# Placing x in a graph network's entry stage: two more blocks before the first layer, behind a wait for all look-ups

## The chip, the cores and the metric

The kernel runs on one core of a Trainium2 chip. The metric is the device time of one execution in microseconds (us), here the median of three runs. The core's engines are TensorE (PE), VectorE (DVE), ScalarE (ACT), GpSimd (POOL) and SyncE (SP); each has an instruction queue of its own, and all wait for each other only through semaphores and at the barrier between two stages.

## What is computed

Four graph convolutions on 50,000 nodes with 96 features, and 50,000 edges sorted by their destination; each is added to its input and layer-normalised. The part that matters here is the first one:

```python
edge_index = jnp.stack([src, dst])
x = _layernorm(x + _L0_gnn_ref(x, L0_gnn_W, L0_gnn_b, src, dst), axis=-1)
...
def _L0_gnn_ref(x, W, b, src, dst):
    inv_sqrt_out = jnp.where(deg_out > 0, jax.lax.rsqrt(deg_out), 0.0)
    inv_sqrt_in = jnp.where(deg_in > 0, jax.lax.rsqrt(deg_in), 0.0)
    h = x @ W
    coef = inv_sqrt_out[src] * inv_sqrt_in[dst]
    msg = h[src] * coef[:, None]
    agg = jax.ops.segment_sum(msg, dst, num_segments=N_NODES)
    return agg + b
```

The three further layers (a max-aggregating pair, a softmax aggregation, an attention layer) are not touched by the change.

## The kernel before, in words

**Tiling.** The 50,000 edges are padded to 128 x 391. A "tile" is one column of 128 edges (or of the 128 node rows that belong to it), a "block" is `Q = 8` tiles; there are `NCH = 49` blocks, 0 to 48 (the last one has 7 tiles), and one extra single-tile block 49 (`FIX`). The big buffer `k.O` holds, for each of the 392 tiles, the node rows of x to which the layer's result is added. A row is placed there by an indirect DMA of POOL, one per tile (128 rows of 384 bytes), with the node numbers in `k.nidx` as its list.

**Stages.** The program is a row of stages: numbering, entry, layer0, layer1 twice, layer2, layer3. Each is a `Block` in which every engine has a program of its own. At a block's end each engine's queue runs a DRAIN instruction and then meets the others at a barrier; no engine starts the next stage before all have arrived. The trace gives these under the line of the stage's `with ctx:` (L527 for entry, L862 for the end of layer0).

**Entry** (from line 512). POOL places blocks 0 to `LATE - 1` = 42 of x in `k.O` (line 642), eight blocks in flight on eight semaphores `placed`. From block `HELD_BACK` = 36 on it first waits until the tallies on PE are done, since the upper part of `k.O` serves as scratch before that: columns of blocks 36 to 42 hold one-hot matrices (`spare`), and those from block 43 up hold `turned_hi`, the transposed one-hot matrices that the look-ups read. A look-up is two matmuls on PE (line 852, reading `turned_hi`) and one instruction on DVE (`look`, line 729) that picks the wanted entries and increments `looked`; there are `2 * TILES` = 128 of them, three behind each of the first 42 blocks that DVE scales and two behind block 42. Meanwhile SP loads each block of x into a ring of four buffers, DVE scales it (line 774), and SP stores it to the table `xs` (lines 615 and 622). SP's program ends when all stores have landed.

**Layer0** (from line 857). POOL first places the blocks that entry left, `LATE` to 49 (line 961), and then gathers the rows of `xs` for the blocks from `RAW` = 8 on into a ring of four slots, one indirect DMA per tile (line 973). Blocks 0 to 7 come by SP from `xraw` (line 937). Before the gathers of block c, POOL waits for what frees its slot:

```python
                if SLOTS <= c < NCH:
                    pool.wait_ge(turned_s, fours(c - SLOTS + 1))
                    pool.wait_ge(counted, c - SLOTS + 1)
                    pool.wait_ge(chained, c - SLOTS + 2)
                    pool.wait_ge(kept[s], 16 * (c // SLOTS))
```

`chained` counts blocks whose running sums are done on DVE (`chain`, line 1004), so `c - SLOTS + 2` means that the chain of block c - 3 has ended; `kept` counts the landed stores of a slot's sums (SP, line 946). DVE's order in each step t is `chain(t)`, then `join(t - 1)` and `factors(t - 1)`. `join` waits for the block's placement (from entry's semaphores below `LATE`, from layer0's above), adds the bias in `k.O` (line 1025), adds PE's product and takes the norm's statistics. From block 8 on a chain begins with line 996, which waits for the block's gathers.

Of the kernel before, what the change touches and what calls it, by code (L numbers as in the profile page):

```python
# [7 lines left out]
F16 = mybir.dt.float16  # L8
# [5 lines left out]
Q = 8  # L14
N_NODES = 50000
N_EDGES = 50000
RAW = 8
LATE = 43
K = 391
KP = K + K % 2  # L20
NP = 128 * K
# [34 lines left out]
def tiles(c):  # L56

    return min(Q, K - c * Q) if c < NCH else 1


def cols(c):
    first = c * Q if c < NCH else FIX
    return slice(first, first + tiles(c))
# [148 lines left out]
def segment_kernel(nc, x, src_k, dst_ext, dst_before, starts, edge_k, W0, b0, W1m, W1e, W1r, b1, W2m, W2e, W2r, b2,  # L212
                   Wg, bg, Wa, att, ba, out):
    ctx = ExitStack()
    with ctx:
# [46 lines left out]
        numbering(nc, k, first, src_k, dst_ext, x, xraw)  # L262
        k.O = sb("O", [128, K + 1, D])
        entry(nc, k, first, x, dst_before, starts, xs)
        layer0(nc, k, second, first, x, xraw, xs, h0, t1, r1, W0, b0, W1m, W1r, b1)
        first.close()
# [245 lines left out]
def entry(nc, k, stage, x, dst_before, starts, xs):  # L512
# [9 lines left out]
    HELD_BACK = 36  # L522
    TILES = RAW * Q
# [3 lines left out]
    with ctx:  # L527
        def sb(name, shape, dt=F32):
            return ctx.enter_context(nc.sbuf_tensor("en_" + name, shape, dt))
# [4 lines left out]
        def sem(name):  # L534
            return stage.sem("en_" + name)
# [22 lines left out]
        table = sb("table", [128, 2, 2, KP], F16)  # L558
        low_bits = sb("low_bits", [128, K], I32)
        y = sb("y", [128, YRING, Q, YW])  # L560
        spare = k.O[:, HELD_BACK * Q:LATE * Q, :].rearrange("p a b -> p (a b)")
        turned_hi = k.O[:, LATE * Q:K, :].rearrange("p a b -> p (a b)")[:, 0:TILES * 64].bitcast(F16)
        halves = lambda at, n: spare[:, at // 2:(at + n) // 2].bitcast(F16)
        width = 2 * HOT * KP
        hots = lambda c: min(HOT, K - c * HOT) if c < NHOT else 1
# [26 lines left out]
        looked = sem("looked")  # L592
# [12 lines left out]
        @block.sync  # L605
        def _(sp):
            sp.dma_start(dprev[:, :], dst_before).then_inc(loaded, 16)
            sp.dma_start(ends[:, 0, :], starts[0:1, :].to_broadcast([128, 128])).then_inc(loaded, 16)
            sp.dma_start(ends[:, 1, :], starts[1:2, :].to_broadcast([128, 128])).then_inc(loaded, 16)

            def load(c):
                u = c % YRING
                if c >= YRING:
                    sp.wait_ge(x_out[u], 16 * (c // YRING))
                sp.dma_start(y[:, u, 0:tiles(c), 0:D], rows(x, c)).then_inc(x_in[u], 16)

            for c in range(YRING - 1):
                load(c)
            for c in range(NCH):
                sp.wait_ge(scaled, c + 1)  # L620
                sp.wait_ge(headed, c + 1)
                sp.dma_start(rows(xs, c), y[:, c % YRING, 0:tiles(c), :]).then_inc(x_out[c % YRING], 16)
                if c + YRING - 1 < NCH:
                    load(c + YRING - 1)
            for u in range(YRING):
                sp.wait_ge(x_out[u], 16 * rounds(NCH, u, YRING))

        @block.gpsimd
        def _(pool):
            pool.memset(after[:, :], 1.0).then_inc(consts, 1)  # L630
            pool.wait_ge(consts, 1)
            pool.affine_select(out=after[:, :], in_=after[:, :], compare_op=ALU.is_gt, fill=0.0,
                               base=0, pattern=[[-1, 128]], channel_multiplier=1).then_inc(consts, 1)
            for c in range(LATE):
                if c >= RING:
                    pool.wait_ge(placed[c % RING], 128 * (c // RING))
                if c == HELD_BACK:
                    pool.wait_ge(s_tallied, NHOT)
                    pool.wait_ge(tallied, NHOT + 1)
                for q in range(tiles(c)):  # L640
                    at = cols(c).start + q
                    pool.indirect_dma_start(k.O[:, at, :], None, x,  # L642
                                            bass.IndirectOffsetOnAxis(k.nidx[:, at:at + 1], 0))\
                        .then_inc(placed[c % RING], 16)
# [212 lines left out]
def layer0(nc, k, stage, old, x, xraw, xs, hist, t1, r1, W0, b0, Wm, Wr, b):  # L857
# [4 lines left out]
    with ctx:  # L862
# [6 lines left out]
        def sem(name):  # L869
            return stage.sem("l0_" + name)  # L870
# [22 lines left out]
        raw_in = [sem(f"raw_in{s}") for s in range(SLOTS)]  # L893
        placed = [k.sem(f"l0_placed{c}") for c in range(LATE, NCH + 1)]
        kept = [sem(f"kept{s}") for s in range(SLOTS)]
# [24 lines left out]
        @block.sync  # L920
        def _(sp):
            clear(sp, old.sems)
            sp.dma_start(w0[:, :], W0).then_inc(weights, 16)
            sp.dma_start(w[0:D, 0:D], Wm).then_inc(weights, 16)
            sp.dma_start(w[0:D, D:2 * D], Wr).then_inc(weights, 16)
            sp.dma_start(w[D:D + 1, D:2 * D], b).then_inc(weights, 16)
            sp.dma_start(b0r[:, :], b0.to_broadcast([128, D])).then_inc(weights, 16)
            raw_rows = xraw.rearrange("(p c q) d -> p c q d", p=128, q=Q)

            def load_raw(c):  # L930
                s = c % SLOTS
                if c >= SLOTS:
                    sp.wait_ge(turned_s, fours(c - SLOTS + 1))
                    sp.wait_ge(counted, c - SLOTS + 1)
                    sp.wait_ge(chained, c - SLOTS + 2)
                    sp.wait_ge(kept[s], 16 * (c // SLOTS))
                sp.dma_start(tile(c)[:, :, 0:D], raw_rows[:, c, :, :]).then_inc(raw_in[s], 16)

            for c in range(SLOTS):
                load_raw(c)  # L940
            for t in range(LAST + 1):
                if t >= 2 and t + 2 < RAW:
                    load_raw(t + 2)
                if t < NCH - 1:
                    sp.wait_ge(chained, t + 1)
                    sp.dma_start(sums_of(hist, t), tile(t)).then_inc(kept[t % SLOTS], 16)
                c = t - 2
                if c >= 0:
                    u, n = c % 2, width(c)
                    sp.wait_ge(taken, c + 1)  # L950
                    sp.dma_start(part_of(t1, c), tr_out[:, u, 0:n, 0:D]).then_inc(stored[u], 16)
                    sp.dma_start(part_of(r1, c), tr_out[:, u, 0:n, D:2 * D]).then_inc(stored[u], 16)
            for u in range(2):
                sp.wait_ge(stored[u], 32 * rounds(NL + 1, u, 2))

        @block.gpsimd
        def _(pool):
            for c in range(LATE, NCH + 1):
                for q in range(tiles(c)):
                    at = cols(c).start + q  # L960
                    pool.indirect_dma_start(k.O[:, at, :], None, x,
                                            bass.IndirectOffsetOnAxis(k.nidx[:, at:at + 1], 0))\
                        .then_inc(placed[c - LATE], 16)
            for c in range(RAW, NL):
# [1240 lines left out]
```

## Time and profile before

| | |
|---|---|
| runs | 3799.91 us median of 3 (3792.94 to 3800.45) |
| the profiled execution | 3788.51 us, of which the span of its instructions is 3786.7 |
| busy over the span | DVE 75%, POOL 71%, PE 49%, ACT 49% |
| entry | from about 157 us to the barrier at 607.7 us |
| layer0 | to the barrier at 1116.4 us |

Times in the rows are microseconds from the span's start, unless marked ns. Register, branch and semaphore instructions don't count as busy; a name with a q (POOLq) is the engine's queue, which runs ahead of the engine. A transfer that POOL issues lands after its row has ended (2.4 to 5.8 us from the issue at line 642).

### The profile page before, as it was taken

To read this page: it belongs to the slowest core of one execution; us is meant where nothing else is said; L and a number is where in the kernel's file an instruction comes from. 1 tells how busy PE (TensorE), PEld (TensorE's weight loads), DVE (VectorE), ACT (ScalarE), POOL (GpSimd) and SP (SyncE) were. 2 spreads that over 40 slices of the span, in tenths; PEclk is the share of its full clock that TensorE was granted. 3 is DMA by queue.
4 is the path that set the end of the run, shared out by engine and by line. 5 is a ranking of instruction groups with operands and counts; after the bars stand their busy time and mean duration, and the time that the engine had idled before them with its cause. 6 is when DMAs were issued, how large, how long until landed. Compare 5 with 4: busy or idle time off the path is not lost. (4 is left out here: it accounts for less than half of the span.)

```text
span 3786.7 us, 39744 instructions
## 1 busy us (share of the span) xinstructions
PE 1847.8 (49%) x8382; PEld 1354.4 (36%) x8382; DVE 2821.7 (75%) x10541; ACT 1853.3 (49%) x3815; POOL 2675.7 (71%) x2760
## 2 busy tenths in 40 slices
PE   5478675888766666744554357888820000000000
PEld 2244313777755555522222157777710000000000
DVE  8899987888866666659999878888755565555555
ACT  8699602776652222225545546666643333333333
POOL 7377776777747777757777477766457777777776
PEclk9899855888878787766666656665655555555555
DMA  2111397666556666646666545555422222222221
GB/s 53 51 41 40 79 295 200 168 166 162 156 139 201 205 205 210 203 131 204 208 202 210 167 156 173 185 171 171 147 82 78 82 77 78 82 74 81 82 73 55
DMA packets 380539, 524.64 MB, mean 139 GB/s; under 512 B 221914, under 2 KB 255983, under 8 KB 380042
## 3 DMA queue, kind: packets, MB, share of 16 engines
q1 hardware_dynamic: 286154, 366.89, 29.3%
q0 software_dynamic: 94144, 155.21, 17.4%
q8 instruction: 69, 1.13, 0.1%
q14 instruction: 172, 1.41, 0.1%
HBM read 230.36 MB, written 291.54 MB: 138 GB/s over the span
## 5 line engine op out<-in xcount | busy, mean ns | idle before, releaser
L1626 POOL DMA_INDIRECT l_G<-t,src x391 | 387.7, 991 | 181.8 <-issue 150.8
L1927 POOL DMA_INDIRECT l_G<-t,src x391 | 373.3, 955 | 168.3 <-issue 107.4
L2161 PE MATMUL l_psR<-l_diag,l_ones 128*128 128x128 f32 x2 | 0.8, 501 | 991.2 <-DVE l_diag L2025 991.2
L1307 POOL DMA_INDIRECT l1a_G<-t,src x391 | 378.8, 969 | 148.3 <-issue 117.3
L1307 POOL DMA_INDIRECT l1b_G<-t,src x391 | 378.4, 968 | 142.8 <-issue 117.9
L1942 POOL DMA_INDIRECT out<-O,nidx x392 | 384.3, 980 | 127.8 <-issue 118.2
L642 POOL DMA_INDIRECT O<-x_pad,nidx x344 | 326.9, 950 | 104.7 <-issue 104.7
L973 POOL DMA_INDIRECT l_G<-xs,src x327 | 311.7, 953 | 99.6 <-issue 96.3
L2161 PEld LDWEIGHTS l_psR<-l_diag,l_ones 128*128 128x128 f32 x2 | 0.5, 310 | 991.3 <-DVE l_diag L2025 991.3
L207 ACT ACTIVATE O<-O,l_shift,l_rstd 128x96 f32<-128x96 f32 x784 | 291.2, 453 | 27.2 <-DVE l_shift L201 26.7
L1480 PE MATMUL l1b_psE<-l1b_G,ident 128*128 128x384 f32 (+1 forms) x198 | 147.1, 845 | 260.3 <-DMA l1b_G<-t,src 260.3
L1982 DVE TENSOR_TENSOR l_e<-l_G,l_to_score 128x8 f32<-128x8 f32 (+3 forms) x51 | 9.3, 183 | 307.6 <-DMA l_G<-t,src 307.6
L1504 PE MATMUL l1a_psP<-l1a_w,l1a_xT 97*128 97x192 f32 x784 | 209.1, 441 | 56.5 <-ACT l1a_xT L1423 56.5
L207 ACT ACTIVATE O<-O,l1b_shift,l1b_rstd 128x96 f32<-128x96 f32 x392 | 146.0, 454 | 162.8 <-DVE l1b_shift L201 162.8
L793 ACT ACTIVATE O<-iota_lo,en_s_from 128x392 f16<-128x392 f16 x391 | 214.1, 654 | 22.8 <-DVE en_s_from L656 22.8
L172 PE MATMUL l_psX<-ident,O 128*96 128x128 f32 x784 | 172.4, 377 | 105.9 <-ACT O L207 82.0
L1504 PEld LDWEIGHTS l1a_psP<-l1a_w,l1a_xT 97*128 97x128 f32 x784 | 189.1, 267 | 73.1 <-ACT l1a_xT L1423 73.1
L2116 ACT ACTIVATE l_psK<-l_dd 128x32 f32<-128x32 f32 (+3 forms) x51 | 10.2, 200 | 371.2 <-DVE l_dd L2002 371.2
L1654 DVE SCALAR_TENSOR_TENSOR l_G<-l_G,cont 128x192 f32<-128x192 f32 x390 | 163.8, 420 | 29.6 <-DMA l_G<-t,src 13.5
L1791 PE MATMUL l_psN<-l_wg,l_vT 97*128 97x96 f32 x784 | 140.2, 352 | 83.5 <-DVE O L1683 60.9
L1480 PEld LDWEIGHTS l1b_psE<-l1b_G,ident 128*128 128x128 f32 x198 | 57.8, 321 | 326.5 <-issue 319.4
L172 PEld LDWEIGHTS l_psX<-ident,O 128*96 128x96 f32 x784 | 124.5, 176 | 133.2 <-ACT O L207 93.2
(351 smaller groups left out, 6480.8 us busy)
## 6 DMA issues: line engine op xcount, KB each, us to landing
h<-l_G SPq DMA_DIRECT2D x96, 392.0 KB, 2.9
t<-l1b_t_out SPq DMA_DIRECT2D x48, 768.0 KB
h<-l_G SPq DMA_DIRECT2D x48, 768.0 KB
xs<-en_y SPq DMA_DIRECT2D x48, 392.0 KB, 4.3
t<-l_t_out SPq DMA_DIRECT2D x48, 392.0 KB, 3.6
l_H<-t SPq DMA_DIRECT2D x48, 392.0 KB, 3.2
en_y<-x_pad SPq DMA_DIRECT2D x48, 384.0 KB, 5.0
t<-l_tr_out SPq DMA_DIRECT2D x48, 384.0 KB
```

The costliest lines, as they stand in the source:

```text
L172: last = pe.transpose(psum[0:D, q * 128:(q + 1) * 128], tile_of(q), ident[:, :])
L207: last = act.activation(out_of(q), tile_of(q), ACT.Identity, bias=shift[:, u, q:q + 1], scale=rstd[:, u, q:q + 1])
L642: pool.indirect_dma_start(k.O[:, at, :], None, x, bass.IndirectOffsetOnAxis(k.nidx[:, at:at + 1], 0))\
L793: made = act.activation(hot_s_lo[:, u, q, :], k.iota_lo[:, :], ACT.Sign, bias=s_from[:, c * HOT + q:c * HOT + q + 1])
L973: pool.indirect_dma_start(tile(c)[:, q, :], None, xs, bass.IndirectOffsetOnAxis(k.src[:, at:at + 1], 0))\
L1307: pool.indirect_dma_start(tile(c)[:, q, :], None, table, bass.IndirectOffsetOnAxis(k.src[:, at:at + 1], 0))\
L1480: pe.matmul(V(c)[:, a:a + n, :], k.ident[:, :], tile(c)[:, a:a + n, :], start=True, stop=False, skip_group_check=True)
L1504: last = pe.matmul(P[:, q, 0:2 * D], xT[:, q * 128:(q + 1) * 128], w[:, :], start=True, stop=True)
L1626: pool.indirect_dma_start(tile(c)[:, q, :], None, table, bass.IndirectOffsetOnAxis(k.src[:, at:at + 1], 0))\
L1654: done = dve.scalar_tensor_tensor(S[:, q, :], before, k.cont[:, at:at + 1], S[:, q, :], ALU.mult, ALU.add)
L1927: pool.indirect_dma_start(tile(c)[:, q, :], None, t4, bass.IndirectOffsetOnAxis(k.src[:, at:at + 1], 0))\
L1942: pool.indirect_dma_start(out, bass.IndirectOffsetOnAxis(k.nidx[:, at:at + 1], 0), k.O[:, at, :], None, bounds_check=NP - 1, oob_is_err=Fa ...
```

## The change

The line between "placed in entry" and "placed in layer0" moves from block 43 to block 45, and the scratch areas keep their old border under a name of their own, `TURNED`. Since blocks 43 and 44 lie on `turned_hi`, POOL waits before block 43 until all 128 look-ups have been counted.

```diff
-LATE = 43
+TURNED = 43
+LATE = 45
...
-        spare = k.O[:, HELD_BACK * Q:LATE * Q, :].rearrange("p a b -> p (a b)")
-        turned_hi = k.O[:, LATE * Q:K, :].rearrange("p a b -> p (a b)")[:, 0:TILES * 64].bitcast(F16)
+        spare = k.O[:, HELD_BACK * Q:TURNED * Q, :].rearrange("p a b -> p (a b)")
+        turned_hi = k.O[:, TURNED * Q:K, :].rearrange("p a b -> p (a b)")[:, 0:TILES * 64].bitcast(F16)
...
                 if c == HELD_BACK:
                     pool.wait_ge(s_tallied, NHOT)
                     pool.wait_ge(tallied, NHOT + 1)
+                if c == TURNED:
+                    pool.wait_ge(looked, 2 * TILES)
                 for q in range(tiles(c)):
```

The same constant `LATE` is the start of layer0's placement loop, the offset of its semaphores `placed`, and the test in `join` that chooses between entry's semaphores and layer0's.

POOL's instructions at the end of entry and the start of layer0, before (O is `k.O`, x_pad is x, and the waits are the semaphores of the kernel's names):

```order
L642 DMA O<-x_pad,nidx 128x96 [waits en_placed2]
L642 DMA O<-x_pad,nidx 128x96 x7
L527 UNCONDITIONAL_BRANCH
L956 UNCONDITIONAL_BRANCH [waits barrier_Pool_Activation_PE_DVE_SP_gather]
L961 DMA O<-x_pad,nidx 128x96 x48
L973 DMA l_G<-xs,src 128x98 [waits l0_chained,l0_kept0,l0_counted,l0_turned_s]
L973 DMA l_G<-xs,src 128x98 x7
```

And of the change, at the same place (its lines stand three further down, those of the stage's end one):

```order
L645 DMA O<-x_pad,nidx 128x96 [waits en_placed2]
L645 DMA O<-x_pad,nidx 128x96 x7
L645 DMA O<-x_pad,nidx 128x96 [waits en_looked,en_placed3]
L645 DMA O<-x_pad,nidx 128x96 x7
L645 DMA O<-x_pad,nidx 128x96 [waits en_placed4]
L645 DMA O<-x_pad,nidx 128x96 x7
L528 UNCONDITIONAL_BRANCH
L959 UNCONDITIONAL_BRANCH [waits barrier_Pool_Activation_PE_DVE_SP_gather]
L964 DMA O<-x_pad,nidx 128x96 x32
L976 DMA l_G<-xs,src 128x98 [waits l0_chained,l0_kept0,l0_counted,l0_turned_s]
L976 DMA l_G<-xs,src 128x98 x7
```

Sixteen placements have moved from behind the barrier to ahead of it, the first of them behind the wait for the look-ups; 48 placements of layer0 have become 32.

## Rows read from the trace of the kernel before

**Rows 1.** Line 527, the end of entry: duration ns min/median/max, start.

```profile
L527 POOLq EVENT_SEMAPHORE  x2: 17/17/17, 607.7 to 607.7; - x2
L527 POOLq DRAIN  x1: 22201/22201/22201, 573.8 to 573.8; - x1
...
L527 DVEq DRAIN  x1: 560/560/560, 605.4 to 605.4; - x1
...
L527 SPq DRAIN  x1: 7/7/7, 607.6 to 607.6; - x1
```

**Rows 2.** Timeline of POOL, end of entry: start, us, instruction [idle before].

```profile
587.86 0.94 POOL L642 DMA_INDIRECT O<-x_pad,nidx  x1 [0.30 <-issue]
608.53 0.94 POOL L961 DMA_INDIRECT O<-x_pad,nidx  x1 [19.73 <-POOLq L527]
```

**Rows 3.** Line 642, 570 to 600 us: duration ns, first and last start.

```profile
L642 POOL DMA_INDIRECT O<-x_pad,nidx x16: 940/944/947, 569.1 to 587.9; - x16
```

**Rows 4.** Timeline of DVE: the last look-up, the last scaling.

```profile
590.41 0.08 DVE L729 DVE_READ_ACCUMULATOR en_picked<-iota_lo,en_s_lo,en_psL 128x1 f32 x1
...
604.35 0.85 DVE L774 TENSOR_TENSOR en_y<-en_y,en_psC 128x672 f32<-128x672 f32 x1 [2.07 <-DMA en_y<-x_pad]
```

**Rows 5.** POOL's other drains: lines 285, 862, 1181 (its second), 1832.

```profile
L285 POOLq DRAIN  x1: 6543/6543/6543, 146.7 to 146.7; - x1
L862 POOLq DRAIN  x1: 4482/4482/4482, 1086.5 to 1086.5; - x1
L1181 POOLq DRAIN  x1: 9701/9701/9701, 2145.1 to 2145.1; - x1
L1832 POOLq DRAIN  x1: 5927/5927/5927, 3780.6 to 3780.6; - x1
L1832 POOLq EVENT_SEMAPHORE  x2: 17/17/17, 3786.6 to 3786.6; - x2
```

**Rows 6.** Timeline of POOL: the last instruction ahead of each of those drains.

```profile
146.93 0.94 POOL L392 DMA_INDIRECT nu_E<-nu_table,nu_first_free  x1 [43.64 <-DMA nu_table<-nu_zero_nodes]
...
1086.73 0.95 POOL L978 DMA_INDIRECT l_F<-h,hrow  x1 [6.19 <-DMA h<-l_G]
...
2145.30 0.94 POOL L1312 DMA_INDIRECT l1b_F<-h1b,hrow  x1 [7.01 <-DMA h1b<-l1b_G]
...
3778.19 0.97 POOL L1942 DMA_INDIRECT out<-O,nidx  x1 [7.48 <-ACT O L207]
```

**Rows 7.** Timeline of POOL: the first gathers of blocks 8, 9 and 10.

```profile
669.54 0.94 POOL L973 DMA_INDIRECT l_G<-xs,src  x1 [0.30 <-PE l_psS L172]
...
679.68 0.95 POOL L973 DMA_INDIRECT l_G<-xs,src  x1 [0.30 <-PE l_psS L172]
...
689.85 0.94 POOL L973 DMA_INDIRECT l_G<-xs,src  x1 [0.30 <-PE l_psS L172]
```

**Rows 8.** Timeline of DVE: the chains of blocks 5 to 9.

```profile
663.28 2.81 DVE L1004 SCALAR_TENSOR_TENSOR l_G<-l_G,cont 128x97 f32<-128x97 f32 x8
...
673.44 2.81 DVE L1004 SCALAR_TENSOR_TENSOR l_G<-l_G,cont 128x97 f32<-128x97 f32 x8
...
683.60 2.81 DVE L1004 SCALAR_TENSOR_TENSOR l_G<-l_G,cont 128x97 f32<-128x97 f32 x8
692.72 0.17 DVE L996 CAST src<-l_G 128x8 int32<-128x8 f32 x1
692.96 2.81 DVE L1004 SCALAR_TENSOR_TENSOR l_G<-l_G,cont 128x97 f32<-128x97 f32 x8
702.09 0.17 DVE L996 CAST src<-l_G 128x8 int32<-128x8 f32 x1
```

**Rows 9.** Line 946, 655 to 690 us: the stores of sums, DMA to landing.

```profile
L946 SPq DMA_DIRECT2D h<-l_G x3: 1263/1406/1468, 658.8 to 677.9; - x3
DMA to landing us min/median/max: 6.7/6.7/6.7
```

**Rows 10.** Waits of POOL in layer0: total us, times, longest.

```profile
POOL l_G L973 <- issue: 96.3, 316, 0.3
POOL O L961 <- POOLq L527: 19.7, 1, 19.7
```

**Rows 11.** Line 973, and what DVE's line 996 waited for (us, times).

```profile
L973 POOL DMA_INDIRECT l_G<-xs,src x327: 940/944/1124, 669.5 to 1079.5; - x164
...
  DMA l_G<-xs,src: 11.9, 10
```

**Rows 12.** Timeline of DVE: its last wait for a gather in layer0.

```profile
1056.84 0.23 DVE L996 CAST src<-l_G 128x8 int32<-128x8 f32 x1 [2.18 <-DMA l_G<-xs,src]
```

## The prediction

> **What bounds the kernel now.** I read the end of entry first, since that is where work is added. The queue instructions of the stage's end [rows 1] show who arrives at the barrier last: SP's drain stands at 607.6 and the barrier opens at 607.7, DVE's drain ends at 606.0 (605.4 + 0.56), and POOL's drain ends at 596.0 (573.8 + 22.2). So SP's last store sets the end of entry, and POOL is 11.6 us early. The timeline of POOL [rows 2] shows the same gap from the engine's side: its last placement ends at 588.8, and it then sits idle for 19.7 us until layer0's first placement at 608.53. The reader should see that these are two different numbers: the engine is free for 19.7 us, but only 11.6 us are left once its queue has drained, because the drain ends 7.2 us behind the last placement (596.0 - 588.8).
>
> Then layer0. POOL issues with no gap but the 0.30 us between two DMAs [rows 10, 11]: 327 gathers from 669.5 to 1079.5 are 1.25 us each, 10.0 us a block. DVE's period is 10.2 us a block while the blocks come from xraw (the chains of blocks 5, 6 and 7 [rows 8]) and 9.4 us once they are gathered (692.72 to 702.09). So POOL has a lead at first and loses 0.6 us of it a block; from the middle of the layer on DVE waits for gathers, 11.9 us in 10 waits [rows 11], the last at 1056.84 [rows 12], close to the layer's end. What makes POOL's stream of gathers earlier against DVE's start of the layer is therefore worth up to 11.9 us, and no more.
>
> **The change part by part.**
>
> *The names.* `TURNED` keeps the scratch areas where they were: nothing.
>
> *The wait for the look-ups.* The last look-up's result is read at 590.41 + 0.08 = 590.5 [rows 4], which is 1.7 us after POOL's last placement of today. The wait holds only what stands behind it on POOL, the 16 moved placements, and nobody in entry waits for these. From the release to the first placement I take 0.5 us, an estimate between the 0.30 of a gap between two DMAs and the 0.8 from the barrier to 608.53 [rows 1, 2].
>
> *Sixteen placements ahead of the barrier.* Sixteen of them start over 18.8 us (569.1 to 587.9 [rows 3]) and the last takes 0.94, so they end at 590.5 + 0.5 + 18.8 + 0.9 = 610.7. That alone is 3.1 us past the 607.6 at which SP arrives. Behind it comes the drain. Its cost is not shown for this place, so I bound it by the drains the trace has [rows 5, 6], each from the end of POOL's last instruction to the end of the drain: 5.4 us after numbering (153.2 - 147.9), 3.3 after layer0 (1091.0 - 1087.7), 8.6 at the second L1181 (2154.8 - 2146.2), 7.3 at the kernel's end (3786.5 - 3779.2), and 7.2 here. I take 7.2, the same queue behind the same kind of placement under the same traffic; the ends are 3.3 and 8.6. The drain does gate the barrier: at the kernel's end POOL's drain ends at 3786.5 and the semaphores follow at 3786.6 [rows 5]. So POOL arrives at 610.7 + 7.2 = 617.9, and layer0 starts 617.9 - 607.6 = **10.3 us later** (6.4 to 11.7). The cover that hid POOL's end, the 11.6 us up to SP's arrival, is used up.
>
> The Trainium skill (PSUM — Partial Sum Buffer, Engine vs sequencer instructions) says that a "drain waits for the engine to go fully idle". Read with POOL's rows alone that would put the arrival at 610.7, and the start 3.1 us later instead of 10.3. The trace disagrees with that reading: the drain ended 7.2 us behind the last row. The Trainium skill (Perfetto Trace Analysis, DMA Instruction — SWDGE) also says that such a row ends when the descriptors are written and not when the data has moved, which fits a tail behind it.
>
> *More traffic beside the last stores of entry.* The 16 transfers run beside SP's last five loads and stores. These may come later, but SP now has 617.9 - 607.6 = 10.3 us of slack: nothing.
>
> *Sixteen placements fewer in layer0.* They free 16 x 1.25 = 20 us of POOL ahead of the gathers. How much of that can be used is set by the slots. Block 8's slot is free once the chain of block 5 has ended, at 663.28 + 2.81 = 666.1 [rows 8] (the store of sums that it also needs was issued at 658.8 and landed 6.7 later, at 665.5 [rows 9]), and its gathers start at 669.54 [rows 7]. With 0.3 us for the release, only 669.5 - 666.4 = 3.1 us can be won; blocks 9 and 10 give the same (679.68 - 676.25 - 0.3 and 689.85 - 686.41 - 0.3). From block 11 on POOL is the slower one again and carries the 3.1 us through to the last wait of DVE, which they shorten, since 3.1 is less than 11.9. The rest of the 20 us becomes a new wait of some 17 us on POOL ahead of block 8. Ends: 0, if the store of sums lands a few us later and frees the slot last, and 3.4, with no release. **I take 3.1 us gained.**
>
> *Blocks 43 and 44 in `join`.* They are joined 400 us later; their placement is hidden either way.
>
> **Sum.** 10.3 - 3.1 = +7.2 us, all of it on the path, since every later stage starts at a barrier. The profiled execution would go from 3788.51 to 3795.7 us; it is 11.4 us below the median of the three runs shown, to which I add the same: 3799.91 + 7.2 = **3807.1 us**, taken as 3807. From the ends, the change is 6.4 - 3.4 = +3.0 to 11.7 - 0 = +11.7 us. About 0.2%, 7.6 us, is what a measurement of this kernel can tell from no change, so the forecast lies just inside it, on the slow side.
>
> **Rivals.**
>
> *The drain has no tail to pay.* If the 7.2 us are a cost of the DMA queue being full of SP's traffic, or pass while POOL sits at the new wait, the start moves by 3.1 only and the sum is 3.1 - 3.1 = 0: 3800 us. For it: the shortest drain shown is 3.3, behind a lone DMA. Against it: the one behind a lone DMA at 2145 took 8.6. With a tail of 3.3 the sum is 6.4 - 3.1 = +3.3, 3803 us; that is the low end of the forecast, not this rival.
>
> *Slower by more.* The gain in layer0 doesn't come. The place is POOL's wait ahead of block 8: the store of sums leaves 0.6 us of room before the chain (665.5 against 666.1 [rows 8, 9]), and it decides from a landing 0.6 us later on; at 3.4 later nothing of the gain is left. With the drain at 7.2 or at 8.6 that is +10.3 or +11.7: 3810 to 3812 us. For it: the small room, three times in a row. Against it: with 16 placements fewer, layer0's first stores meet less traffic.
>
> *Faster.* The gathers come early enough that DVE never waits: -11.9 us. With a start 3.1 us later that is -8.8, 3791 us. It needs POOL to begin block 8 some 12 us before the chain of block 5 ends, which the wait on `chained` excludes, unless the chains themselves come earlier. Against it: DVE is busy through the first eight blocks and does not wait for POOL there. With the full 10.3 it would be -1.6, no change.
>
> *The change doesn't do what it says.* If `looked` reached 128 well before 590, the 16 placements would join the others at 588.8 and end 1.9 us earlier: +5.3, 3805 us. The timeline of DVE excludes it, for the last look-up ends at 590.5.
>
> **How the numbers follow.** The forecast (+3 to +9) has a chance of 0.68, of which 0.31 lies above 7.6 us, since two of the five drains shown would put it there or next to it; no tail 0.12; slower by more 0.14; faster 0.04; the last 0.02. Slower by over 0.2%: 0.31 + 0.14 = 0.45. Faster by over 0.2%: 0.05, the rival's 0.04 and a little scatter. Within 0.2%: the other 0.50. The range starts at 3797 (no tail, on a run at the low end of the three shown) and ends at 3813 (drain 8.6, no gain, and 1 us of the runs' own scatter).
>
> **What the profile after would show.** Right: a gap of about 2 us on POOL ahead of the first placement of block 43 at 591; POOL's last placement ending at 610.7; its drain ending at about 618 and all other queues waiting for it; layer0's first instructions 10 us later; a wait of some 17 us on POOL ahead of block 8; DVE's waits for gathers down from 11.9 to about 9 us; the barrier behind layer0 at 1116.4 + 7.2 = 1123.6. Wrong: the barrier still at 608 to 611 (no tail), the first gather of block 8 more than 1 us after the end of the chain of block 5 (no gain), or a stage after layer0 whose length has changed.

## The result, and the profile after

The change makes the kernel slower: 3806.7 us median of 9 runs (3802.8 to 3812.48), the kernel before 3796.58 us median of 9 (3789.46 to 3800.45). The ratio is 1.0028 with a 95% interval of 1.0018 to 1.0038, so between 6.8 and 14.4 us of 3797; the difference of the medians is 10.1 us. The profiled execution took 3802.8 us, with a span of 3801.0 from its first instruction to its last.

The end of entry (line 528 of the changed kernel) answers to [rows 1]; columns are duration ns min/median/max, first and last start:

```profile
L528 POOLq EVENT_SEMAPHORE  x2: 17/17/17, 619.4 to 619.4; - x2
...
L528 POOLq DRAIN  x1: 21022/21022/21022, 598.3 to 598.3; - x1
...
L528 DVEq DRAIN  x1: 669/669/669, 605.1 to 605.1; - x1
...
L528 SPq DRAIN  x1: 7/7/7, 607.7 to 607.7; - x1
```

SP arrives at 607.7, 0.1 us from where it was. POOL's drain now ends at 598.3 + 21.0 = 619.3, and the barrier opens at 619.4, 11.7 us later than before. The timeline of POOL answers to [rows 2, 7]; columns are start, duration, instruction, [idle time before <- what ended it]:

```profile
591.04 0.95 POOL L645 DMA_INDIRECT O<-x_pad,nidx  x1 [1.69 <-DVE en_picked L732]
...
609.81 0.94 POOL L645 DMA_INDIRECT O<-x_pad,nidx  x1 [0.30 <-issue]
620.21 0.95 POOL L964 DMA_INDIRECT O<-x_pad,nidx  x1 [9.46 <-POOLq L528]
...
678.85 1.03 POOL L976 DMA_INDIRECT l_G<-xs,src  x1 [18.19 <-PE l_psS L173]
...
688.99 1.05 POOL L976 DMA_INDIRECT l_G<-xs,src  x1 [0.35 <-PE l_psS L173]
```

The first moved placement starts at 591.04, 0.8 us behind the end of the last look-up (590.26), and the last one ends at 610.75, as the sum had it. The drain then takes 8.6 us more, not 7.2. In layer0 the 20 us that POOL was relieved of turn into a wait of 18.2 us ahead of block 8. The chains on DVE answer to [rows 8]:

```profile
675.18 2.81 DVE L1007 SCALAR_TENSOR_TENSOR l_G<-l_G,cont 128x97 f32<-128x97 f32 x8
...
685.34 2.81 DVE L1007 SCALAR_TENSOR_TENSOR l_G<-l_G,cont 128x97 f32<-128x97 f32 x8
```

The chain of block 5 ends at 677.99 and that of block 6 at 688.15, and the gathers of blocks 8 and 9 follow 0.86 and 0.84 us behind them: the slots gate POOL now. (The row of the first gather names PE's `l_psS` as what ended the wait. That is inferred. In e3, below, the same wait is put down to the chain on DVE, the distance is 0.85 us, and PE's work on `l_psS` was still running when the gather started.) Against the barrier, the first gather of block 8 comes at 678.85 - 619.4 = 59.4 us, before at 669.54 - 607.7 = 61.8. So 2.4 us of 20 are won. DVE sees nothing of it until block 25, the first whose gathers it had to wait for before. The row is the start of that block's chain (line 996, now 999), before and after:

```profile
855.13 0.39 DVE L996 CAST src<-l_G 128x8 int32<-128x8 f32 x1 [1.51 <-DMA l_G<-xs,src]
```

```profile
865.38 0.17 DVE L999 CAST src<-l_G 128x8 int32<-128x8 f32 x1
```

Counted from the barrier that is 247.4 us before and 246.0 after: the wait is gone, and the chain starts 1.4 us earlier. At the last block's chain the lead is 1.3 us. The gather stream and the end of layer0 answer to [rows 11]:

```profile
L976 POOL DMA_INDIRECT l_G<-xs,src x327: 943/947/1124, 678.9 to 1089.9; - x164
```

```profile
DVE src L999 <- DMA l_G<-xs,src: 11.4, 12, 2.1
```

```profile
L865 POOLq EVENT_SEMAPHORE  x2: 17/17/17, 1126.9 to 1126.9; - x2
```

The last gather starts 10.4 us later than before and the barrier behind layer0 opens 10.5 us later (1126.9 against 1116.4). The code behind this barrier is the same in both kernels. The later barriers of the two profiled executions lie +9.2, +7.6, +12.5 and +14.2 us apart (1649.4 against 1640.2 for the first, the end of the program for the last); they scatter both ways about the 10.1 us that the medians show, and nothing is to be explained there from one execution of each.

### The profile page after: what moved, and what is told of

Its sections match the earlier page's. It is cut to its first block and busy times, and to the rows that moved or that the text cites. A ratio compares the mean times of both kernels' runs of the same rounds, so it can differ in the third digit from the quotient of the medians.

```text
span 3801.0 us, 39745 instructions
## 1 busy us (share of the span) xinstructions
PE 1841.3 (48%) x8382; PEld 1348.9 (35%) x8382; DVE 2824.9 (74%) x10541; ACT 1853.4 (49%) x3815; POOL 2678.3 (70%) x2760
## 5 line engine op out<-in xcount | busy, mean ns | idle before, releaser
L645 POOL DMA_INDIRECT O<-x_pad,nidx x360 | 342.8, 952 | 111.0 <-issue 109.3
L1507 PE MATMUL l1a_psP<-l1a_w,l1a_xT 97*128 97x192 f32 x784 | 201.0, 428 | 56.8 <-ACT l1a_xT L1426 56.8
L2119 ACT ACTIVATE l_psK<-l_dd 128x32 f32<-128x32 f32 (+3 forms) x51 | 10.2, 200 | 372.3 <-DVE l_dd L2005 372.3
L1155 PE MATMUL l_psP<-l_w,l_xT 97*128 97x192 f32 x784 | 167.6, 374 | 7.4 <-ACT l_xT L1092 7.2
```

The costliest lines, as they stand in the source:

```text
L645: pool.indirect_dma_start(k.O[:, at, :], None, x, bass.IndirectOffsetOnAxis(k.nidx[:, at:at + 1], 0))\
L1155: last = pe.matmul(P[:, q // 2, q % 2 * 2 * D:(q % 2 + 1) * 2 * D], xT[:, c % 2, q * 128:(q + 1) * 128], w[:, :], start=True, stop=True)
L1507: last = pe.matmul(P[:, q, 0:2 * D], xT[:, q * 128:(q + 1) * 128], w[:, :], start=True, stop=True)
```

## The experiments

The theory is the prediction's: POOL's drain gates the barrier, and the ring of four slots limits what can be won in layer0. The first four kernels take cost, gain and size apart; e5, e8 and e9 move placements to where the drain stays hidden, and e6 to e9 open the slots; e10 asks what the drain waits for. In the table, "barrier" is the end of entry, "gather 8" the first gather of block 8 counted from it, and "layer0" the time from that barrier to the next, all from the one profiled execution of each. Each ratio is against runs of the kernel before that were made beside it; their medians lie between 3791.9 and 3796.8 us.

| kernel | time against before (95%) | barrier | gather 8 | layer0 |
|---|---|---|---|---|
| before | 1 | 607.7 | 61.8 | 508.7 |
| the change | 1.0028 (1.0018 to 1.0038) | 619.4 | 59.4 | 507.5 |
| e1, one block | 0.9998 (0.9987 to 1.0008) | 608.7 | 59.8 | 507.9 |
| e2, cost alone | 1.0021 (1.0011 to 1.0032) | 619.8 | 61.6 | 510.0 |
| e3, gain alone | 0.9986 (0.9976 to 0.9996) | 607.2 | 59.3 | 509.5 |
| e4, three blocks | one run, 3814.55 us | 630.0 | 59.1 | 507.2 |
| e5, eight hidden | 1.0006 (0.9996 to 1.0016) | 608.0 | 59.5 | 513.9 |
| e6, five slots | 1.0005 (0.9995 to 1.0014) | 605.9 | 62.1 | 513.0 |
| e7, change and five slots | 0.9997 (0.9988 to 1.0006) | 619.2 | 49.2 | 500.7 |
| e8, hidden and five slots | 0.9983 (0.9973 to 0.9992) | 605.7 | 51.8 | 506.9 |
| e9, the same, other scratch | 0.9976 (0.9967 to 0.9986) | 606.3 | 51.9 | 501.7 |
| e10, landings awaited | one run, 3806.08 us | 620.0 | 59.8 | 508.1 |

**e1, one block instead of two**

```diff
-LATE = 45
+LATE = 44
```

> One block (8 placements) moves ahead of the barrier instead of two; the wait for the look-ups stays. Theory (POOL's drain gates the barrier, the slots limit the gain): POOL's last placement ends at about 601, its drain ends 7.2 to 8.6 us later, at 607.9 to 609.3, so the barrier opens 0.3 to 1.7 us later than before; the gathers of block 8 again start right behind the chain of block 5, which gives back 2.4 us. Sum -2.1 to -0.7 us, no change that can be measured. Rival (the placements slow SP's last stores and the first loads of layer0): SP's drain moves to 609 or later and half of the +10 us of the change remains, +5 us.

```profile
L528 POOLq DRAIN  x1: 14472/14472/14472, 594.1 to 594.1; - x1
...
L528 SPq DRAIN  x1: 7/7/7, 607.3 to 607.3; - x1
```

POOL's last placement ended at 600.7 and its drain at 608.6, 7.9 us later, 1.3 us behind SP. The barrier opened 1.0 us later than in the trace of before, inside the theory's 0.3 to 1.7; SP was not slowed (607.3), which the rival needed. The first gather of block 8 came 2.0 us earlier against the barrier, where 2.4 was expected. The time is that of the kernel before: the interval is 4.9 us less to 3.0 us more, which leaves out the rival's +5.

**e2, the cost alone**

```diff
+REST = 43
...
-            for c in range(LATE, NCH + 1):
+            for c in range(REST, LATE):
+                pool.wait_ge(k.early_placed[c % 8], 128 * (c // 8 + 1))
+            for c in range(REST, NCH + 1):
```

> Entry as in the change; layer0 places all of blocks 43 to 49 as the kernel before did, so blocks 43 and 44 are placed twice and POOL has nothing less to do there. Theory: barrier as in the change, 11.7 us later than before, and no gain: the first gather of block 8 comes 11.7 us later, +11.7 us in all. Rival (the cost arises inside layer0, from having the placements gone from there): no more than 5 us of it is left.

The barrier opened at 619.8 and the first gather of block 8 started at 681.4, 61.6 us behind it, as in the kernel before. The whole time is 1.0021 of before, 4.2 to 12.2 us more by the interval, which holds the +11.7 of the theory near its upper end: the cost is there with all of layer0's placements in place, and so arises in entry. The rival falls: at most 5 us of 10 were to remain, and the barrier alone is 12 us late.

**e3, the gain alone**

```diff
-        placed = [k.sem(f"l0_placed{c}") for c in range(LATE, NCH + 1)]
+        placed = [k.sem(f"l0_placed{c}") for c in range(REST, NCH + 1)]
...
-            for c in range(LATE, NCH + 1):
+            for c in range(REST, NCH + 1):
```

with `REST = 45` beside `LATE = 43`, and `join` not waiting for blocks 43 and 44.

> Entry as in the kernel before; layer0 places only blocks 45 to 49. This leaves out the placement of blocks 43 and 44, whose rows of x are missing from the result. Theory: barrier at 607.7 as before; POOL has 20 us less to do and turns 17 to 18 us of it into a wait ahead of block 8, whose gathers start about 0.85 us behind the chain of block 5, 2.4 us earlier than before: -2.4 us. Rival (the slots don't limit it, and POOL's time ahead of the gathers comes off DVE's 11.9 us of waits): -11.9 us.

```profile
666.53 1.04 POOL L974 DMA_INDIRECT l_G<-xs,src  x1 [18.19 <-DVE l_G L1005]
```

The same wait of 18.2 us appears with entry untouched, and gather 8 comes 2.5 us earlier against the barrier. The interval of the times, 0.9976 to 0.9996, is a gain of 1.5 to 9.1 us; it holds the 2.4 of the theory and not the 11.9 of the rival. The profiled layer0 was not shorter, though (509.5 against 508.7 us), so the gain that reaches the end of the layer is shown by the times and not by this trace.

**e4, three blocks**

```diff
-LATE = 45
+LATE = 46
```

> Three blocks (24 placements) ahead of the barrier. Theory: 10.0 us more than the change, all of it on the barrier and none given back: POOL's last placement ends at 620.7, its drain at 627.9 to 629.3, and the first gather of block 8 comes 19 to 20 us later than before. Rival (the drain's tail is room that a longer wait fills, or the gain grows with the placements moved): less than 8 us more than the change.

```profile
L528 POOLq DRAIN  x1: 24196/24196/24196, 605.7 to 605.7; - x1
```

The drain ends at 629.9, 9.2 us behind the last placement (620.7), and gather 8 starts at 689.1, 19.5 us later than before. A third block costs 10.6 us at the barrier, of which 9.9 are its placements and the rest a longer drain, and gains nothing more in layer0. Its one time, 3814.55 us, is 7.9 above the change's median, just under the rival's 8; one run does not decide that, but the barrier does.

**e5, eight placements where the drain stays hidden**

```diff
+HIDDEN = list(range(387, 392)) + list(range(344, 347))
...
+            for at in HIDDEN:
+                if at == LATE * Q:
+                    pool.wait_ge(looked, 2 * TILES)
+                pool.indirect_dma_start(k.O[:, at, :], None, x, bass.IndirectOffsetOnAxis(k.nidx[:, at:at + 1], 0))\
+                    .then_inc(hidden, 16)
```

> Eight placements move ahead of the barrier, but such that POOL's drain ends before SP arrives: first tiles 387 to 391, which lie beyond turned_hi and need no wait, then, behind the wait for the look-ups, tiles 344 to 346. Theory: POOL's last placement ends at 598.5, its drain at 605.7 to 607.7, the barrier opens at 607.7 as before, and block 8's gathers start 2.4 us earlier: -2.4 us, which the times can hardly show. Rival (any placement beside SP's last stores costs): barrier at 609 or later.

POOL's drain ended at 606.8 (590.7 + 16.1) and SP arrived at 607.9, so the barrier cost nothing, and gather 8 came 2.3 us earlier. Yet the time is that of before: the interval is 1.5 us less to 6.1 us more, and leaves out the 2.4 us less that the theory expected. The profiled layer0 was 5 us longer. In that execution the 5 us lie in its tail, from about 1094 us, where the last small blocks are chained, to the barrier. The row of a stretch is us, busy time and (count) of PE, PEld, DVE, ACT and POOL, granted clock, DMA share and GB/s; first the kernel before, then e5:

```profile
1094.00:1116.00 22.00, 13.83 (x74) 11.36 (x72) 11.94 (x59) 14.32 (x39) 0.00 (x0) 0.86 0.42 109
```

```profile
1094.00:1121.00 27.00, 22.05 (x76) 18.57 (x74) 10.25 (x50) 12.91 (x33) 0.00 (x0) 0.50 0.33 87
```

```profile
DVE O L1050 <- PE l_psN L1158: 8.7, 4, 3.4
```

About the same matmuls (74 and 76) kept PE busy for 13.8 us at a granted clock of 0.86 and for 22.1 us at 0.50, the 1.2 GHz level. DVE waits for PE in this tail (8.7 us in e5, 1.4 in the kernel before). Whether the clock of this stretch goes with the kernel or with the execution is open: e5 and e8 had 0.50 in their profiled execution, e6 and e7 0.73, and e9, which has e8's order of work, 0.82. So this accounts for the one profiled execution; that it is also why the eleven runs of e5 show no gain is not shown.

**e6 and e7, five slots, without and with the change.** In both (and in e8) three small tiles of layer0 overwrite the table `next_same`, which layer3 still reads, so layer3 computes other scores with the same instructions.

```diff
-    SLOTS = 4
+    SLOTS = 5
...
-                if t >= 2 and t + 2 < RAW:
-                    load_raw(t + 2)
+                if t >= 2 and t + SLOTS - 2 < RAW:
+                    load_raw(t + SLOTS - 2)
```

> The kernel before with five slots in layer0 instead of four (three small tiles of layer0 lie in a table that is no longer used, so that it fits). Theory: block 8 may start behind the chain of block 4, at about 656.6, but POOL has 48 placements to issue until 669.5, so nothing changes: 0 us, gathers of block 8 at 669.5. Rival (the ring of slots holds the kernel back by itself): -5 us or more.

> The change with five slots in layer0. Theory: the barrier opens 11.7 us late as in the change, and the first gather of block 8 comes 0.85 us behind the chain of block 4, 12.5 us earlier against the barrier than in the kernel before; DVE's 11.9 us of waits for gathers all but vanish, so layer0 is 11 to 12 us shorter: 11.7 - 11.5 = about 0 us in all. Rival (something other than the slots kept the 20 us of POOL from being used): layer0 as long as in the change, +9 us.

```profile
668.42 1.04 POOL L976 DMA_INDIRECT l_G<-xs,src  x1 [7.87 <-PE l_psS L173]
```

```profile
DVE src L999 <- DMA l_G<-xs,src: 2.4, 1, 2.4
```

Five slots alone change nothing that the times show (1.0005; the interval leaves out the rival's -5 us; gather 8 at 62.1 us). With the change, gather 8 comes 49.2 us behind the barrier, 12.6 us earlier than before, DVE's waits for gathers fall from 11.4 to 2.4 us, and layer0 takes 500.7 us against the change's 507.5 (though its tail had a lower clock, 0.73 against 0.87 over the last 41 to 45 us). Against the kernel before, layer0 is 8.0 us shorter where 11 to 12 were expected, so that 3.5 us of the late barrier are left at its end in this execution. The times show none of it: the whole is 0.9997 of before, 4.6 us less to 2.3 us more. So the slots were what kept the 20 us from being used.

**e8 and e9, hidden placements and five slots.** e8 is e5 with e6's edit. e9 puts the small tiles into the table `restart`, which layer1 computes anew:

```diff
-        b0r = sb("b0r", [128, D])
+        b0r = k.restart[:, 290:290 + D]
...
+                dve.tensor_scalar(k.restart[:, :], k.cont[:, :], -1.0, BIG, ALU.add, ALU.mult)
+                dve.drain()
```

> Eight hidden placements and five slots together. Theory: barrier at 607.7; POOL has 40 placements to issue in layer0, which take it to 658.5, behind the end of the chain of block 4 (655.8), so the gathers of block 8 start at 658.5 instead of 669.5 and layer0 becomes 10 to 11 us shorter: -10.5 us, 0.28% faster than before. Rival (DVE's waits for gathers have another cause, such as the gathers' landing): -3 us or less.

> Eight hidden placements and five slots, now with layer0's three small tiles in the table restart (which layer1 computes anew at its start) instead of next_same, which layer3 still reads. Theory: as in e8, barrier at 606 to 608, first gather of block 8 about 51 us behind it, layer0 shorter by 10 us in its gathers; the end of layer0 is 4 us shorter or longer by the clock that PE is granted there. -6 to -10 us, faster than both kernels. Rival (e8's -0.17% came from the wrong table): 0 us.

```profile
L528 POOLq EVENT_SEMAPHORE  x2: 17/17/17, 606.3 to 606.3; - x2
...
L528 POOLq DRAIN  x1: 16852/16852/16852, 589.4 to 589.4; - x1
...
L528 SPq DRAIN  x1: 7/7/7, 605.7 to 605.7; - x1
```

```profile
L982 POOL DMA_INDIRECT l_G<-xs,src x327: 943/947/1124, 658.2 to 1069.8; - x164
```

e9 computes the whole kernel at 0.9976 of before (0.9967 to 0.9986), about 9 us faster (5 to 12.5 by the interval), and so beats both: its barrier is at 606.3, its first gather comes 9.9 us earlier against the barrier than that of the kernel before, and its layer0 is 7.0 us shorter. With eight placements the drain is just at the edge: it ended at 606.25, 0.6 us behind SP. e8's time is 0.9983 of before, 3.0 to 10.2 us less, so the expected 10.5 was missed by a little, and the rival's "-3 us or less" is only just outside. The intervals of e8 and e9 overlap, and no difference between the two is shown by the times. In the profiled executions e8's tail ran at the low clock (layer0 506.9 against 501.7 us).

**e10, the landings awaited**

```diff
+            for c in range(TURNED, LATE):
+                pool.wait_ge(placed[c % RING], 128 * (c // RING + 1))
+            pool.memset(after[0:1, 0:1], 0.0)
```

> The change, with POOL waiting at the end of entry until its last 16 placements have landed, and then doing one small memset, so that the drain follows that. The last placement is issued at 609.8 and lands 2.4 to 5.8 us later. If the drain's tail runs from the last DMA whatever comes after it (a wait for that DMA's own end and clean-up), the drain still ends 8.6 us behind the last placement's row, at 619.3, and the barrier does not move against the change. If the tail is charged anew behind the last instruction of POOL, the drain ends at 621 or later.

```profile
608.72 0.94 POOL L645 DMA_INDIRECT O<-x_pad,nidx  x1 [0.30 <-issue]
611.26 0.09 POOL L650 MEMSET en_after<- 1x1 f32 x1 [1.59 <-DMA O<-x_pad,nidx]
```

```profile
L528 POOLq DRAIN  x1: 8656/8656/8656, 611.2 to 611.2; - x1
```

The last 16 transfers had landed by 611.2, POOL had nothing left but a memset of 0.09 us, and the drain still took 8.7 us from there, to 619.9. It ended 10.2 us behind the last DMA's row and not 8.6, and 8.5 us behind the memset's. The times of the expectation, 619.3 and "621 or later", fit neither way as they stand, since this execution ran 1.1 us early (last placement at 608.72 against 609.81) and the landings took only 1.6 us from the end of the last row. Counted from its own rows, a tail behind the last DMA would have ended at 609.7 + 8.6 = 618.3, and one behind the last instruction at 611.35 + 8.6 = 619.9, where it did end. So, as far as one execution shows, the tail is no wait for the transfers: it is charged anew behind POOL's last instruction.

**The drain over all kernels.** The time from the end of POOL's last instruction in entry to the end of its drain, by the number of placements in that stage:

| placements in entry | drain's tail, us |
|---|---|
| 344 | 7.20 (before), 7.23 (e3), 7.25 (e6) |
| 352 | 7.87 (e1), 7.95 (e8), 7.94 (e9), 8.57 (e5) |
| 360 | 8.57 (the change), 8.60 (e2), 8.54 (e7), 8.51 (e10, behind its memset) |
| 368 | 9.24 (e4) |

The tail repeats to 0.1 us in kernels with the same count, e5 apart, and is about 0.7 us longer with each block of eight placements more. So most of its spread is no scatter between executions. Whether the number of placements sets it, or something that goes with it, no run here separates.

## Why the prediction was right or wrong, point by point

**The end of entry.** Right in mechanism. POOL was free for 19.7 us but had only 11.6 before SP's arrival, and the drain decides; the placements ended at 610.75 against 610.7. That they agree so closely is luck in part: the last look-up ended 0.2 us earlier than in the kernel before, and the release took 0.8 us and not 0.5. The term "drain, 7.2" was mis-sized: it measured 8.6, the upper of the two ends given. The prediction took it as unchanged by the change, "the same queue behind the same kind of placement"; it was 7.2 to 7.3 us with entry's old 344 placements and 8.5 to 8.6 with the change's 360. The start of layer0 moved 11.7 us and not 10.3. The rival without a tail fell, and so did the reading of the Trainium skill's sentence (PSUM — Partial Sum Buffer, Engine vs sequencer instructions) in which the engine's last row marks its being idle; 610.8 would have been the arrival by it.

**More traffic beside the last stores.** Right: SP's drain stood at 607.7 in the change and at 607.3 to 607.9 in e1, e2, e4 and e5.

**The slots and the gain.** Right: 18.2 us of POOL's time became a wait, and e3 and e7 show the gate from both sides. The term "0.3 us for the release" was too small; it measured 0.86, and the chain of block 5 itself ended 0.2 us later against the barrier, so the gain was 2.4 us and not 3.1. (POOL's pace is 10.06 us a block by the rows, 410.0 / 326 x 8, so it loses 0.7 us a block to DVE and not 0.6; nothing hangs on this.) That POOL carries the lead to where DVE waits for it was right too; the meeting is at block 25. Of the 2.4 us the profiled execution kept 1.2 at the end of layer0. Its gathers had a median of 947 ns against 944, which over 327 of them is 1.0 us; since all of e1 to e4, run together, had 947 and all of e5 to e8 had 944, it goes with the set of runs and not with the kernel.

**The waits of DVE.** Forecast at about 9 us, found at 11.4. The waits partly come at other blocks, so their sum is no measure of the gain; the slower gathers explain 1.0 us of the difference, and the rest stays open.

**The sum.** 11.7 - 2.4 = 9.3 by the measured terms, 10.1 by the medians, where +7.2 was forecast; both terms erred to the same side, by 1.4 and 0.7. As a difference the result lies outside the forecast of +3 to +9, though inside the +3.0 to +11.7 of its ends, and at 10.1 it is over the 7.6 us that the forecast lay just below (its interval, 6.8 to 14.4, begins under them). As a time it lies in the middle of the range, 3797 to 3813, and that is luck. The predicted 3807 us and the measured 3806.7 agree more closely than they should: the median of nine runs of the kernel before is 3.3 us under the median of three from which it started.

**The rival "slower by more".** Its size, +10.3 to +11.7, nearly came true, but not by its cause: the slot was not freed late by a store of sums, since the gathers followed the chain by 0.86 us; the drain's tail was longer.

## What to carry to other kernels

An engine that sits idle before a stage's barrier has less room than its timeline shows: behind its last instruction comes the drain, here 7 to 9 us on POOL at this barrier, and what is put there must end that much before the slowest engine. The tail read from one trace is not a constant either: here it grew by 0.7 us with each block that was put ahead of it. Ask also what the freed time will meet downstream: 20 us taken off POOL ahead of its gathers started them 2.4 us earlier with four slots and 12.6 with five. Both limits have to move together, as in e9; each alone (e5 and e6) gave nothing that the times show.

## What had not been expected of the hardware

POOL's drain is no wait for the landing of its DMAs: with its last 16 transfers landed and one memset of 0.09 us behind them, it still took 8.7 us (e10). It grew with the placements in the stage, from 7.2 us at 344 of them to 9.2 at 368. What it does in that time stays open. And the clock granted to TensorE in the short tail of layer0 goes with about half of what the change costs: 0.86 or 0.50 over the same 75 or so matmuls, 13.8 or 22.1 us of busy time, and a layer0 of 508.7 or 513.9 us (the kernel before and e5).
